# Two attention stages of a cross attention model reordered: feed forward spread over the turns, output product halved, product with the values behind the scores

## What is computed

```
for each of 6 layers, x of one batch is 512 x 256:
    q, k, v = split(x @ Wqkv)                      # 16 heads of 64, 512 tokens
    q, k = l2norm and rotary(q), l2norm and rotary(k)
    window of 64 queries looks at its own and the previous 64 keys
    out = softmax(8 * q @ k.T + mask) @ v
    x = x + out @ Wo
    a, gate = split(layernorm(x) @ W1 + b1)        # 682 columns each
    x = x + (a * gelu(gate)) @ W2 + b2
result = x0 + tanh(g) * x
```

## Time and profile before

| | |
|---|---|
| runs | 4918.86, 4923.18, 4928.29 us |
| median | 4923.18 us |
| profiled execution | 4925.18 us, its span 4923.6 us |
| TensorE (PE) busy | 4627.5 us, 94% |
| VectorE (DVE) busy | 3525.2 us, 72% |
| ScalarE (ACT) busy | 3126.4 us, 63% |
| GpSimd (POOL) busy | 2539.9 us, 52% |
| chain that ended last | PE 64%, DVE 12%, ACT 9%, POOL 8%, issue 5% |
| instructions | 92149 |

### The profile page before, as it was taken

One profiled execution on the slowest core, in us unless ns is written; L12 is line 12 of the kernel. 1 busy time (PEld: TensorE's weight loads), 2 busy tenths in 40 slices (PEclk: granted clock), 3 DMA queues, 4 the chain that ended last, 5 costly groups with the idle time before them and its releaser, 6 DMA issues.

```text
span 4923.6 us, 92149 instructions
## 1 busy us (share of the span) xinstructions
PE 4627.5 (94%) x34664; PEld 2932.9 (60%) x34664; DVE 3525.2 (72%) x6388; ACT 3126.4 (63%) x7586; POOL 2539.9 (52%) x2346
## 2 busy tenths in 40 slices
PE   6899999999999999969999999999999999999998
PEld 2233333344444343247777777777787877778776
DVE  4766666766575767758777777777777777777775
ACT  3566566555555556547767677767777676777674
POOL 3222211112122122068777778787778787877773
PEclk8999999999999999989999999999999999999999
DMA  4323322332222223111111111111111111111110
GB/s 119 63 49 61 73 41 56 72 59 47 61 52 60 56 44 72 25 56 47 32 36 40 36 37 40 34 43 34 35 37 44 37 40 31 42 34 35 44 38 31
DMA packets 178922, 233.02 MB, mean 47 GB/s; under 512 B 29648, under 2 KB 121424, under 8 KB 178256
## 3 DMA queue, kind: packets, MB, share of 16 engines
q1 hardware_dynamic: 178480, 227.14, 20.6%
HBM read 150.09 MB, written 32.51 MB: 37 GB/s over the span
## 4 chain that ended last, share of the span: by engine, by line
PE 64%; DVE 12%; ACT 9%; POOL 8%; issue 5%; DMA 1%; SPq 0%; DVEq 0%; POOLq 0%; ACTq 0%
PE psum L1410 13%; PE psum L1454 9%; PE psum L522 6%; PE psum L508 5%; PE psum L487 5%; PE psum L1462 3%; ACT lprobs L1724 3%; PE psum L1496 3%; PE psum L1486 3%; DVE maxes L712 2%; PE psum L469 2%; PE psum L1477 2%; POOL stats L1782 2%; PE psum L511 2%; PE psum L477 1%
## 5 line engine op out<-in xcount | busy, mean ns | idle before, releaser
L918 ACT ACTIVATE probs<-psum 128x1024 f32<-128x1024 f32 x768 | 779.0, 1021 | 639.7 <-PE psum L508 391.3
L712 DVE TENSOR_REDUCE maxes<-psum 128x1 f32<-128x1024 f32 x512 | 615.4, 1211 | 299.5 <-PE psum L487 296.0
L1724 ACT ACTIVATE lprobs<-psum,small_stats,stats 128x128 f32<-128x128 f32 x1536 | 687.3, 474 | 40.1 <-DVE small_stats L1611 39.2
L1782 POOL TENSOR_TENSOR stats<-stats,minus_half 128x8 f32<-128x8 f32 x384 | 651.2, 1696 | 32.0
L1454 PE MATMUL psum<-wqkv_hi,xs_hi 128*128 128x512 f32 (+1 forms) x1536 | 549.4, 358 | 31.5 <-POOL xs_lo L1769 27.3
L1778 POOL TENSOR_TENSOR lwork<-lwork 128x512 f32<-128x512 f32 x384 | 501.4, 1306 | 110.6 <-DVE lwork L1595 110.6
L508 PE MATMUL psum<-stack 98*128 98x512 bf16 x1536 | 503.4, 383 | 30.5 <-DVE maxes L712 19.4
L1454 PE MATMUL psum<-wqkv_lo,xs_hi 128*128 128x512 f32 (+1 forms) x1536 | 520.3, 339 | 0.0
L1454 PE MATMUL psum<-wqkv_hi,xs_lo 128*128 128x512 f32 (+1 forms) x1536 | 519.8, 338 | 0.0
L487 PE MATMUL psum<-stack 96*128 96x512 bf16 x1536 | 465.2, 385 | 44.2 <-ACT probs L918 34.4
L1593 DVE TENSOR_TENSOR lwork<-psum,rotary 128x512 f32<-128x512 f32 x384 | 264.2, 688 | 299.6 <-PE psum L1454 203.4
(11 more groups left out here) (242 smaller groups left out, 11101.8 us busy)
## 6 DMA issues: line engine op xcount, KB each, us to landing
mixed_vals<-vals SPq DMA_DIRECT2D x672, 64.0 KB, 2.0
stack<-k_parts SPq DMA_DIRECT2D x288, 128.0 KB
staged<-in_quads SPq DMA_DIRECT2D x144, 256.0 KB, 3.0
k_parts<-parts SPq DMA_DIRECT2D x48, 384.0 KB, 2.9
stack<-q_parts SPq DMA_DIRECT2D x288, 64.0 KB
staged<-in_w SPq DMA_DIRECT2D x54, 256.0 KB, 3.0
ctx<-in_ctxT SPq DMA_DIRECT2D x24, 512.0 KB, 5.3
q_parts<-parts SPq DMA_DIRECT2D x24, 384.0 KB, 3.3
```

The source lines that it names most:

```text
L712: ins = vector.tensor_reduce(to, pair(("M", u)), AX.XY, ALU.max)
L918: scalar.activation(probs[:, i % 6, :, :], pair(("E", u)), ACT.Exp).then_inc(S_["E_act"], 1)
L1724: ins = scalar.activation(pr[:, h, :], scores(u)[:, h % 2, h // 2, :], ACT.Exp, bias=st[:, 4 + h:5 + h], scale=y[:, h:h + 1], accum_out=st ...
L1782: pool_step(gpsimd.tensor_tensor(st[:, 8:16], st[:, 0:8], minus_half[:, :], ALU.pow))
```

## The change

In the last part: the order of groups and batches in a half layer becomes (group, batch) (0,0), (1,0), (1,1), (0,1), (2,0), (3,0), (3,1), (2,1), and likewise for the other two batches, so that the first batch of a half is done two units ahead of its end. The feed forward's steps are put at other turns. `wo` is cut in two steps, one for each half of the output channels, at the end of one turn and in the next; its additions become a step `wx` of their own, behind `dv`. Inside a turn `pv` comes behind the scores (and `wo`), ahead of `tr`, and `pt` follows `tr` on TensorE. Loads of weights are put at other turns, chunks of one group one turn apart, and the feed forward waits for the chunks that it reads instead of for all. In the first part: inside a turn `E` and then `M` come first, but `E` comes last in the turn behind a GELU; and where a turn holds none of a list of steps, the exponential of `E` is two instructions, the first of which already frees half of the bank pair.

```diff
-    return Order(p for t in sorted(turn) for p in turn[t])
+    gelu_turns = {t for t in turn for p in turn[t] if p[0] == "gl"}
+    def place(t):
+        late = 3 if t - 1 in gelu_turns else 0
+        return sorted(turn[t], key=lambda p: {"E": late, "M": 1}.get(p[0], 2) if t >= 0 else 2)
+    busy = {"PV", "pj", "va", "wp", "wo", "f0a", "f0p", "f0b", "m1", "ep", "s2p", "s2", "t2", "v2p", "v2", "k2", "r2", "r3"}
+    order = Order(p for t in sorted(turn) for p in place(t))
+    order.halved = [p[1] for t in sorted(turn) for p in place(t) if p[0] == "E" and not busy & {q[0] for q in turn[t]}]
+    return order
...
+        def pair_left(key, i):
+            before = two[key][1]
+            if before:
+                before = first_half.get(before, before) if i == 0 else before
+                PE.wait_ge(S_[before[0]], before[1])
...
+                    if u in order.halved:
+                        scalar.activation(probs[:, i % 6, 0, :], pair(("E", u))[:, 0, :], ACT.Exp).then_inc(S_["Eh_act"], 1)
+                        scalar.activation(probs[:, i % 6, 1, :], pair(("E", u))[:, 1, :], ACT.Exp).then_inc(S_["E_act"], 1)
...
-    units = [(d, g if h == 0 else 3 - g, 2 * h + b) for d in range(DEPTH) for h in range(2) for g in range(4) for b in range(2)]
+    halves = [((0, 0), (1, 0), (1, 1), (0, 1), (2, 0), (3, 0), (3, 1), (2, 1)), ((2, 2), (3, 2), (3, 3), (2, 3), (0, 2), (1, 2), (1, 3), (0, 3))]
+    units = [(d, g, b) for d in range(DEPTH) for half in halves for g, b in half]
     for d in range(DEPTH):
-        for n, t in enumerate((31, 32, 34, 35, 37, 38, 39, 40, 42)):
-            load(64 * d + t if d else 2 + 2 * n, 0, ("f", d), [n])
-        put(64 * d - 44 if d else -1, ("rt", d))
-        for b, t in enumerate((-3, 3, 29, 35)):
-            put(64 * d + t if d or b > 1 else -2, ("xs", (d, b)))
+        t0 = 64 * d
+        for key, q, o in (((0, 0), -4, 5), ((0, 1), 0, 9), ((0, 2), 12, 21), ((0, 3), 16, 25), ((1, 0), 44, 53), ((1, 1), 48, 57)):
+            load(t0 + q if t0 + q >= 0 else -2, 1 if t0 + q >= 0 else 0, ("q", d) + key, range(3))
+            load(t0 + o, 1, ("o", d) + key, range(1))
+        for t, j in ((27, 0), (28, 3), (30, 1), (31, 4), (35, 2), (36, 5), (38, 6), (39, 7), (40, 8)):
+            load(t0 + t, 0, ("f", d), [j])
+        put(t0 - 44 if d else -1, ("rt", d))
+        for b, t in enumerate((-3, 6, 29, 38)):
+            put(t0 + t if d or b > 1 else -2, ("xs", (d, b)))
...
-        put(4 * n + 11, ("wo", (d, g, b)))
+        for m in range(C):
+            put(4 * n + 10 + m, ("wo", (d, g, b, m)))
+            put(4 * n + 11, ("wx", (d, g, b, m)))
     for d in range(DEPTH):
         for b in range(B):
-            r = 64 * d + 32 * (b // 2) + 38 + 13 * (b % 2)
-            norm = [r - 2, r - 1, r, r + 1, r + 2, r + 3, r + 4]
-            steps = [r + 6 - b % 2 + i for i in (0, 1, 2, 4, 5, 6, 8, 9, 10)]
+            t0 = 64 * d + 32 * (b // 2)
+            norm = (32, 34, 35, 36, 37, 38, 39) if b % 2 == 0 else (49, 50, 51, 52, 53, 54, 55)
+            gates, linear, second = ((40, 44, 48), (41, 45, 50), (49, 52, 53)) if b % 2 == 0 else ((56, 60, 64), (57, 61, 66), (65, 68, 69))
+            if d == DEPTH - 1 and b == B - 2:
+                gates, linear, second = (40, 42, 44), (41, 43, 45), (46, 47, 48)
+            elif d == DEPTH - 1 and b == B - 1:
+                norm, gates, linear, second = (40, 41, 42, 43, 44, 46, 46), (47, 49, 51), (48, 50, 52), (53, 54, 55)
...
-    rank = {st: i for i, st in enumerate(("wo", "mv", "sc", "tr", "rot", "pv", "dv", "ex", "pt"))}
-    rank.update({"qkv": 20, "lq": 21})
-    return Order(p for t in sorted(turn) for p in sorted(turn[t], key=lambda p: rank.get(p[0], 10 if t >= 0 else 30)))
+    rank = {st: i for i, st in enumerate(("fo", "mv", "sc", "wo", "pv", "tr", "rot", "dv", "ex", "pt", "wx"))}
+    rank.update({"qkv": 30, "lq": 32})
+    def place(t, p):
+        if t < 0:
+            return 40 if p[0] not in rank else rank[p[0]]
+        return 31 if p[0] == "wo" and p[1][3] == 0 else rank.get(p[0], 20)
+    return Order(p for t in sorted(turn) for p in sorted(turn[t], key=lambda p: place(t, p)))
```

More of the change, by code:

```diff
@@ L412, in left @@
                 waits.wait_ge(S_[before[0]], before[1])
+        first_half = {("E_act", order.nth["E", u]): ("Eh_act", n + 1) for n, u in enumerate(order.halved)}
+        def pair_left(key, i):
[3 more added lines that the diff above has]
+                PE.wait_ge(S_[before[0]], before[1])
         at_ = order.at
@@ L1226, in last_order @@
             for t, stage in zip(norm, ("fo", "fa", "fq", "fb", "fy", "fc", "fd")):
-                put(t, (stage, (d, b)))
+                put(t0 + t, (stage, (d, b)))
             for j in range(HT // 2):
-                put(steps[2 * j], ("hg", (d, b, j)))
-                put(steps[2 * j + 1], ("ha", (d, b, j)), ("hm", (d, b, j)))
-            for i, t in enumerate(steps[HT:]):
-                put(t, ("fw", (d, b, i)), *([("fx", (d, b, i - 1))] if i else []))
+                put(t0 + gates[j], ("hg", (d, b, j)))
@@ L1233, in last_order @@
+                put(t0 + linear[j], ("ha", (d, b, j)), ("hm", (d, b, j)))
+            for i, t in enumerate(second):
+                put(t0 + t, ("fw", (d, b, i)), *([("fx", (d, b, i - 1))] if i else []))
             if d == DEPTH - 1:
-                put(steps[HT], ("kb", b))
-                put(steps[HT + 2] + 1, ("fin", b))
-    rank = {st: i for i, st in enumerate(("wo", "mv", "sc", "tr", "rot", "pv", "dv", "ex", "pt"))}
-    rank.update({"qkv": 20, "lq": 21})
-    return Order(p for t in sorted(turn) for p in sorted(turn[t], key=lambda p: rank.get(p[0], 10 if t >= 0 else 30)))
+                put(t0 + second[0], ("kb", b))
+                put(t0 + second[2] + 1, ("fin", b))
@@ L1335, in last_part @@
         any_ = [()]
[L1336 removed]
+        last_use = {weights_of(*p[1][:3]): p[1][:3] for p in order.parts if p[0] == "wo"}
         wqkv_at = plan(order, range(2), lambda p: [p[1][1:4]] if p[0] == "lq" and p[1][0] == "q" and p[1][4] == 0 else [],
@@ L1388, in stat, with loaded @@
             return stats[:, stat_at[name, u][0], :]
-        def loaded(key, j):
-            return at_("lq", key + (j,))
+        def loaded(key, *chunks):
+            return max(at_("lq", key + (j,)) for j in chunks)
         def chunk(u):
@@ L1505, in tensor_program @@
                     wh, wl = wout_hi[:, wout_at[w][0], :], wout_lo[:, wout_at[w][0], :]
-                    for m in range(C):
-                        left(one, ("wo", u, m), PE)
-                        for k in range(2):
-                            w0 = k * D + m * P
-                            ins = three(bank(("wo", u, m)), wh[:, w0:w0 + P], wl[:, w0:w0 + P], att_hi[:, k, :], att_lo[:, k, :], k == 0, k == 1)
+                    left(one, ("wo", u), PE)
+                    for k in range(2):
+                        w0 = k * D + m * P
+                        ins = three(bank(("wo", u)), wh[:, w0:w0 + P], wl[:, w0:w0 + P], att_hi[:, k, :], att_lo[:, k, :], k == 0, k == 1)
                     ins.then_inc(S_["add_pe"], 1)
```

57 lines of the change are left out of this document (25 added, 32 removed).

## The result

The changed kernel takes 4811.84 us (median of four runs, 4807.02 to 4811.94) against 4922.45 us for the kernel before, beside which it was timed: a ratio of 0.9772, 95% interval 0.9755 to 0.9789. The forecast was 4788 us, with a range of 4735 to 4852. The profiled execution has a span of 4810.6 us, 113.0 less than before.

What follows compares the result with a forecast made beforehand. TensorE's own instruction stream was taken as the limit, so only its idle time and hidden steps could be won. Terms -119 - 37 - 4 - 7 + 50 - 18 = -135 us, from 4923.2 to 4788 us; 8-in-10 range 4735 to 4852.

Steps and rivals of the forecast that it cites:

- A: Last part: moving the feed forward, cutting wo and preparing norm sums and x's halves earlier removes TensorE's waits; -119 us.
- E: Last part: new waits, from exponentials behind both copies, PSUM banks and things unseen; +50 us (0 to +100).
- B: Last part: pv directly behind the scores saves a tile shape change, 0.13 us in 288 turns; -37 us (-23 to -49).
- the sign of being wrong that I had named: Last part: qkv or feed forward waiting in every turn for VectorE's low half of pv or ScalarE's square; no size.
- D: Tail: the schedule ends four turns earlier, so half of the remaining idle time goes; -7 us (-11 to 0).
- C: Start of the last part: respaced and later weight loads shorten the wait for transposed keys; -4 us (-7 to +3).
- F: First part: moving E and M and cutting exponentials shortens waits for exponentials and maxima; -18 us (-40 to +15).
- The first: Last part: nearly all waits go and no new one comes; 4733 us (4715 to 4755), chance 0.12.
- the third: Last part: feed forward waits only move to other turns; 4864 us, up to 4900, chance 0.06.
- the second: Last part: exponentials' chain returns in both wo turns of four, VectorE reducing late; 4846 us (4822 to 4880), chance 0.13.
- The fourth: Last part: PSUM banks rotate in fixed order, TensorE waits each turn for pv's low half; 5018 us, chance 0.03.
- The fifth: Last part: each table load costs 1.4 us more, lengthening 72 turns behind a GELU; +36 us, 4824, chance 0.01.

Runs made afterwards that it cites:

- The banks swapped: Changed kernel, but of qkv's two PSUM banks the values' bank returns to the rotation first, the bank awaiting ScalarE's square second; 4785.50 us, ratio 0.9718.
- the experiment with the exponentials ahead: Changed kernel, but ScalarE does the exponentials ahead of the copies of pv and tr in turns with wo's second half; 4907.31 us, ratio 0.9971.
- the kernel without the halves: Changed kernel, but the first part's 158 cut exponentials stay whole; 4816.73 us, ratio 0.9781.
- E never last: Changed kernel, but in the first part E stays ahead also in the 16 turns a layer pass behind a GELU; 4815.48 us, ratio 0.9785.
- M not ahead: Changed kernel, but in the first part M is not moved ahead of PV and of the reciprocals; 4812.23 us, ratio 0.9776.

## Why the prediction was right, and where it was not

**A, the waits: right in cause, too large.** A count per turn gives the sizes. TensorE's own length of a turn is 4.41 with nothing on top (before 4.55), 7.13 with a piece of twelve matmuls (7.29), 6.00 with wo's second half. What the turns are longer than this was about 126 us before and is about 63 after: -63, where A and E together said -119 + 50 = -69. With the turns moved and neither order nor cut, the same count leaves 41: -85 instead of -119. So A was too large by some 34 us, and the order and the cut added the other 22. In its reading of the earlier trace rows the prediction let the chain begin with VectorE's addition; as said above, ScalarE's copies and table load held that turn, and the addition did not.

**B, the order: right in size, but half of it is paid back.** TensorE's own work fell by about 33 us (forecast 37), and another 4 us of pieces left these turns for the tail. In the changed kernel scores to pv is 0.67 us, pv to tr 0.61, and both groups of transpositions take 0.85: at turn 20

```profile
3307.56 0.30 PE L1511 MATMUL psum<-band_bias,ident_b 64*64 64x256 bf16 x4
3307.69 0.61 PE L1516 MATMUL psum<-keys,queries 64*64 64x128 f32 x16
3308.23 0.34 PE L1535 MATMUL psum<-turned,mixed_vals 128*64 128x64 f32 x4
...
3308.84 0.66 PE L1501 MATMUL psum<-ident,lwork 128*128 128x128 f32 x4
3309.34 0.60 PE L1525 MATMUL psum<-ident,lprobs 128*128 128x128 f32 x4
3309.69 0.48 PE L1449 MATMUL psum<-hid_hi,w_hi 128*128 128x512 f32 x1
```

3309.69 - 3308.84 = 0.85 for eight transpositions. What I counted apart, as E, comes with it: turned back, the order is worth 17 to 19 us of turns, and alone, in the kernel before, nothing (1.0004).

**E, the new waits: near in sum (63 against 50), half of it in another place.** The chain of the turns with wo's second half was forecast at 6.12 us against 5.93 of TensorE, with the exponentials behind both copies. It measured 6.18 against 6.00. The trace, for the turn whose scores begin at 3356.45:

```profile
3358.70 0.34 PE L1535 MATMUL psum<-turned,mixed_vals 128*64 128x64 f32 x4
...
3359.32 0.66 PE L1501 MATMUL psum<-ident,lwork 128*128 128x128 f32 x4
3359.43 0.38 ACT L1773 ACTIVATE att_hi<-psum 128x256 fp32r<-128x256 f32 x1 [0.87 <-PE psum L1535]
...
3360.01 0.38 ACT L1748 ACTIVATE queries<-psum 128x256 f32<-128x256 f32 x1 [0.20 <-PE psum L1501]
...
3360.61 0.47 ACT L1760 ACTIVATE lprobs<-psum,small_stats,stats 128x128 f32<-128x128 f32 x1
...
3362.63 0.30 PE L1511 MATMUL psum<-band_bias,ident_b 64*64 64x256 bf16 x4
```

tr at 2.87 (2.80), its copy at 3.56 (3.49), the exponentials at 4.16, the next scores 2.02 later at 6.18; TensorE's work is 6.00. 96 x 0.18 = 17 us (forecast 16). The first turns, without feed forward, lose 12 (16), and their plain length is the forecast chain, 4.60 (4.61). The PSUM banks lose about 31 us at turns 4, 9, 17, 20, 24 and 25, where I had 10: I had seen one case, the GELU product behind a norm step, and not that the second feed forward product and tr meet the square's bank too. The steps that were too small are the +10 for the banks and "for what I have not seen, +8", together 18 against 31. The banks swapped show the cause for turns 4, 17, 20 and 24, which make 22 of the 31; for 9 and 25, which got longer by that edit, the row of pt and the GELU does. ScalarE's square did show as what the feed forward waits for, the sign of being wrong that I had named, though in 17 waits (9.8 us) and not in every turn.

**D, the tail: wrong sign.** +6.9 instead of -7, 14 us, the largest share of the 22 us between the forecast and this execution. I took half of the idle time as gone because the schedule ends four turns earlier. TensorE's busy time from turn 384 on is 80.5 us before and 85.7 after, idle 15.7 and 17.4. The same work ends in fewer turns: 532 of TensorE's matmuls stand there instead of 515, 17 x 0.23 = 3.9 us that stood in turns 4 to 383 before. Three waits of the chain are as long as before or longer (2.79, 1.09 and 2.60 us there), and more matmuls ran at the lower clock, as the last section tells. With the same last part, two other kernels ended in 100.1 us, so that about +4 is the change's and about 3 the lower clock's in this execution. The row that answers to the earlier trace rows, and two others:

```profile
4732.04 0.34 PE L1535 MATMUL psum<-turned,mixed_vals 128*64 128x64 f32 x4 [2.78 <-issue]
...
4744.47 0.50 PE L1449 MATMUL psum<-att_hi,wout_hi 128*128 128x512 f32 x1 [1.44 <-DVE att_lo L1660]
...
4750.63 0.80 PE L1449 MATMUL psum<-xn_hi,w_hi 128*128 128x512 f32 x1 [3.11 <-DVE xn_lo L1688]
```

The last one was 2.60 and is 3.11. Fewer turns are no shorter tail if the chain of the last batch (pv, wo, norm, first product) keeps its length.

**C and F.** C -3.7 (-4). F -16 (-18), a sum that came out right by luck, of steps that were sized wrongly: the halves win 5 to 8 us where I had a cost of 3, E's late place 4 to 5 instead of 8, M's place nothing instead of 13. I priced M's earlier start by the wait that it shortens, and did not ask what M itself waits for once it comes earlier.

**The rivals.** The first (all waits go, none comes) and the third (they only move) are both excluded by the count of 63 us of 126. Of the second, half the condition is seen: the chain came back in one turn of four, not in two. The fourth did not happen, and its mechanism is the one that costs 31 us here and has the largest wait, 41 us, in the experiment with the exponentials ahead. The fifth did not happen: the turns 1, 13 and 29, in each of which ScalarE computes a GELU and loads a table, are 7.13 as TensorE's work alone is (turn 1 is 7.28 in every other half layer); 9, 17 and 25 are longer, which the banks explain.

## What to carry to other kernels

Where products rotate over few PSUM banks in the order of the program, look for the reader that comes last, and hand its bank on last: two lines of code gave 18 us of turns here, as much as the order of pv and tr (18.6); then look again, since another product now gets the bank of the next late reader. A wait that an earlier start shortens is a gain only if what starts earlier has nothing to wait for itself; price a step with the chain of its engine in the turns that have a GELU or a norm on top, not in a plain one. And count the tail by its chain and its matmuls, not by the number of turns.

## What the runs showed of the hardware

The granted clock falls to its lower level in the tail, but not after each wait of this kind. Windows (columns as in the earlier trace rows); of the changed kernel:

```profile
4732.00:4736.00 4.00, 3.96 (x27) 3.34 (x28) 1.80 (x4) 1.85 (x4) 1.28 (x1) 0.61 0.01 4
4742.00:4750.60 8.60, 4.09 (x32) 2.89 (x30) 7.43 (x10) 3.00 (x4) 1.70 (x1) 0.96 0.22 75
4750.60:4755.00 4.40, 4.37 (x10) 3.51 (x11) 0.00 (x0) 0.00 (x0) 0.00 (x0) 0.50 0.30 95
```

Of the kernel without the halves, whose last part is the same, behind the same wait of 3.11 us:

```profile
4759.70:4764.10 4.40, 4.38 (x19) 3.64 (x20) 0.00 (x0) 1.27 (x2) 0.00 (x0) 1.00 0.35 104
```

And of the kernel before, behind its waits of 0.73 and 2.60 us:

```profile
4852.00:4856.00 4.00, 3.84 (x30) 2.45 (x32) 1.08 (x3) 1.04 (x3) 0.00 (x0) 0.57 0.45 130
4868.00:4872.00 4.00, 3.89 (x11) 3.14 (x12) 1.25 (x3) 2.43 (x3) 1.28 (x1) 0.65 0.00 0
```

In the changed kernel the granted clock is 0.61 behind 2.78 us of idle time and 0.50 behind 3.11 (0.50 is 1.2 GHz). Matmuls that stand 0.23 us apart elsewhere stand 0.43 apart there, so that 10 of them are under way in the 4.4 us where the kernel without the halves has 19. With the same last part and the same wait of 3.11 us, the clock stayed at 1.00 in two of the four executions (without the halves, E never last) and fell to 0.50 in the other two (the changed kernel, M not ahead). Their ends from turn 384 on are 100.1 and 100.1 us against 103.1 and 104.6. So a wait of this length in the tail cost its own length, or that and about 3 us more, and no run here shows what decides it. The prediction had it at its length alone, and the kernel before had such stretches too.
